# Attention scores on TensorE: three bf16 parts against two float32r parts, and the constant fills moved

## The chip, the cores and the metric

The kernel runs on one core of a Trainium2 chip. The metric is the device time of one execution in microseconds (us). TensorE (PE) does matrix products, VectorE (DVE) and ScalarE (ACT) do elementwise work and reductions and read TensorE's results from PSUM, GpSimd (POOL) does elementwise work and issues the indirect transfers, and SyncE (SP) issues nearly all other DMAs, one after the other in the order of its program.

## The reference

One layer on x of 4 x 1024 x 128 (float32): half a mixture of experts, attention, and half the same mixture again.

```python
x = x + 0.5 * ffn(layernorm(x), W1, b1, W2, b2, Wr, br)      # top-1 of 8 experts
x = x + attn(layernorm(x), Wq, bq, Wk, bk, Wv, bv, Wo, bo)   # 16 heads of 8
x = x + 0.5 * ffn(layernorm(x), W1, b1, W2, b2, Wr, br)

def attn(x, ...):
    q = (x @ Wq + bq).reshape(B, S, 16, 8).transpose(0, 2, 1, 3)   # k and v alike
    scores = einsum('bhsd,bhtd->bhst', q, k) / sqrt(8)
    ctx = einsum('bhst,bhtd->bhsd', softmax(scores), v)
    return ctx.transpose(0, 2, 1, 3).reshape(B, S, 128) @ Wo + bo
```

The softmax needs each row's maximum before its exponentials; the kernel computes all scores twice, once for the maxima and once for the exponentials.

## The kernel before

Five stages follow each other: the front (norm, routing of the 4096 tokens to experts, `Front`), the first expert stage (`Tiles`: 32 tiles of 128 sorted tokens, gathered and scattered by GpSimd's indirect DMAs), attention (`attention`), and routing and experts again.

**Precision.** A matmul of bf16 keeps 8 bits of a number, so query and key are each cut into three bf16 parts (`PARTS = 3`). All nine products of parts are summed in one matmul by putting them side by side on the contracted rows: 9 x 8 = 72 rows (`ROWS`) for one head. The maxima use 64 of them (`MAX_ROWS`); the exponentials' scores use 72, and two more rows, the guards, that hold minus the maximum of the query's row in two parts, against ones in the key's tile. For even heads of a group the rows start at partition 0 and the score matmul contracts 74 rows; for odd heads the maxima's rows start at 64 and the score matmul contracts all 128 rows, where the spare rows are constants: zeros in the query's tile `q2`, ones in the key's `k2`. Those constants, and ones in the value tile `vs`, are written by 12 memsets on GpSimd (`gpsimd_fill`, 4 for each of 3 buffers), one behind each of the first 12 scatters of the first expert stage.

**Making the parts.** Tokens come in 8 quads of 512. For each quad and for query and key ACT writes the first part (`high_part`), DVE or POOL the remainder (`remainder`, `remainders`), ACT the second part (`second_part`), DVE or POOL the third (`third_part`). SP stores them in HBM (`store_query`, `store_key`), the key's three times over, and loads them again per group of 4 heads (`load_queries`, `load_keys`, 10 DMAs a group). The parts of a quad live in one of `SPLITS = 3` buffers; ACT's `high_both(q)` waits until the stores of quad q - 3 have landed.

**The softmax.** There are 16 groups of 4 heads (`GROUPS`), each with 16 steps, 256 steps in all. In a step PE does two maxima units (each two matmuls of 512 columns into one `ps_m` bank pair, on rows 0-63 and 64-127), scores 0, 1 and 2 of the step (into the three banks `ps_s`), the values of the step before (four f32 matmuls of 32 output partitions each, into `ps_o`), and score 3. DVE reduces each maxima unit (`maxima_unit`), ACT does four exponentials. The maxima run 22 units ahead (`AHEAD`), so units for a later half stand in each of the first 245 steps, and the first 22 units are done in the prologue, among the projections of the quads (`prologue`). Score n waits until exponential n - 3 has freed its bank; a maxima unit waits until the unit two before it is reduced; the values of a step wait for all four exponentials of it.

**Guards.** After 16 units (a half of a group, 8 steps) the maxima go round: DVE `combine`, POOL `split_maxima`, DVE `turn_maxima` (behind the second unit of the next half), then SP `place_guard`: a DMA to HBM, a wait for it to land, and two DMAs into `q2`. PE waits for them (`in_m`) at the start of each eighth step, ahead of that step's first unit. Which rows the names mean: `ps_m<-k,q` are maxima units, `ps_s<-q,k` scores, `ps_o<-probs,vs` values.

Of the kernel before, what the change touches and what calls it, by code (L numbers as in the profile page):

```python
# [4 lines left out]
F32 = mybir.dt.float32  # L5
BF16 = mybir.dt.bfloat16
I32 = mybir.dt.int32
# [6 lines left out]
P = 128  # L14
# [21 lines left out]
PARTS = 3  # L36
ROWS = PARTS * PARTS * DK
MAX_ROWS = ROWS - DK
GUARDS = 2
SCORED = ROWS + GUARDS  # L40
# [70 lines left out]
class Setup:  # L111
# [69 lines left out]
    FILLED = 4 * BUFS  # L181
    PAIR = float(0x3f803f80 - 0x3f800000) / 2 ** 23 + 1.0

    def gpsimd_fill(self, pool, n):

        p, piece = n // 4, n % 4
        if n:
            pool.wait_ge(self.filled, n)
        if piece == 0:
            self.nc.gpsimd.memset(self.k2[p][64:96, 0::2, :].bitcast(F32), self.PAIR).then_inc(self.filled, 1)  # L190
        if piece == 1:
            self.nc.gpsimd.memset(self.k2[p][0:64, 1::2, :].bitcast(F32), self.PAIR).then_inc(self.filled, 1)
        if piece == 2:
            self.nc.gpsimd.memset(self.q2[p][0:64, 1::2, :].bitcast(F32), 0.0).then_inc(self.filled, 1)
        if piece == 3:
            self.nc.gpsimd.memset(self.vs[p][:, :, :, :], 1.0).then_inc(self.filled, 1)
# [241 lines left out]
class Front:  # L438
# [121 lines left out]
    def gpsimd(self, pool):  # L560
        self.setup.gpsimd_masks(pool)
        for q in self.BY_POOL:
# [4 lines left out]
            last.then_inc(self.normed_pool, 1)  # L567
        pool.wait_ge(self.route.stored, 2 * 16 * QUADS)
# [3 lines left out]
class Tiles:  # L572
# [68 lines left out]
    def gpsimd(self, pool):  # L641
# [246 lines left out]
SPLITS = 3  # L888
# [59 lines left out]
def attention(nc, w, dram, q2, k2, vs, v_sb, ctx_sb, front, tiles, routes_2):  # L948
# [9 lines left out]
    with ExitStack() as ctx:  # L958
# [10 lines left out]
        exact, rem = probs[:, :, 0:2, :], probs[:, :, 2:4, :]  # L969
# [3 lines left out]
        parts = sb("parts", [P, SPLITS, 2, PARTS, HALF], BF16)  # L973
        parts_flat = parts[:, :, :, :, :].rearrange("p a j m c -> p (a j m c)")
# [8 lines left out]
        split = sb("split", [P, 2, GUARDS, GH // 2 * QUAD], BF16)  # L983
        blocks = [sb(f"blocks{p}", [P, 4 * KT], BF16) for p in range(2)]
# [17 lines left out]
        x_loaded, middle, query_stored, normed_act = tiles.setup.x_load, sem("middle"), sem("query_stored"), front.normed_act  # L1002
        left, low = sems("left", FIRST + 1), sems("low", FIRST + 1)
        LAST = QUADS - 1

        LOADS, STORES = 2 * PARTS + 1 + 3, 1 + PARTS

# [6 lines left out]
        def product(j, n, m=0):  # L1014

            row = (n * PARTS + m) * DK
            return row if j == 0 else MAX_ROWS + row if row < MAX_ROWS else row - MAX_ROWS

        def guard(j):
# [804 lines left out]
```

## Time and profile before

| what | value |
|---|---|
| device time, median of 3 runs | 999.62 us (999.19 to 999.98) |
| span of the profiled execution | 996.9 us (the profile gives this execution's span; its own time is not listed apart from the three above, whose median is 2.7 us above the span) |
| PE, DVE, ACT, POOL busy | 91%, 83%, 75%, 22% of the span |
| largest groups | DVE reductions of maxima 602.8 us, ACT exponentials 555.9 us, PE scores 294.5 us, PE values 272.7 us, PE maxima 159.9 us |

A busy share says only how full an engine is; which one sets the pace has to be read from what each engine waits for in the stretch in question.

### The profile page before, as it was taken

What the parts mean: (1) busy time and instruction counts of PE and PEld (TensorE: products, weight loads), DVE (VectorE), ACT (ScalarE), POOL (GpSimd) and SP (SyncE); (2) the same over time, 40 slices, a digit from 0 to 9 for tenths busy, and PEclk for the clock granted to TensorE, in tenths of its full rate; (3) what the DMA queues carried; (4) which work ended last, traced back from release to release, by engine and by line L of the source; (5) the groups of instructions that cost most, each with busy time, mean ns of one, the idle gap of its engine ahead of it and who ended that gap; (6) DMA issues with size and microseconds to landing.
All of it is one profiled execution on the core that took longest, in us unless ns stands there. A gap on an engine that the chain in (4) does not pass through costs nothing. (4 is left out here: it accounts for less than half of the span.)

```text
span 996.9 us, 18005 instructions
## 1 busy us (share of the span) xinstructions
PE 907.5 (91%) x5949; PEld 385.6 (39%) x6023; DVE 832.2 (83%) x1404; ACT 750.2 (75%) x1507; POOL 219.1 (22%) x317
## 2 busy tenths in 40 slices
PE   5799927899999999999999999999999999965996
PEld 4699923322222222222222222222222222434996
DVE  6776628989999999999999999999999998768664
ACT  4367706978888888888888888888888888754774
POOL 3168841831000000000000100000100000024775
PEclk9989957999999999999999999999999999996998
DMA  7632135752220213202022120220202000051311
GB/s 262 194 96 73 41 116 190 238 192 63 58 61 16 62 34 81 62 17 62 15 73 74 31 62 15 73 54 28 75 30 64 29 23 17 2 169 48 105 63 44
DMA packets 65443, 75.14 MB, mean 75 GB/s; under 512 B 12896, under 2 KB 43784, under 8 KB 65352
## 3 DMA queue, kind: packets, MB, share of 16 engines
q1 hardware_dynamic: 58776, 60.98, 20.6%
q0 software_dynamic: 5120, 12.59, 4.1%
q8 instruction: 51, 0.84, 0.3%
q10 hardware_dynamic: 1456, 0.41, 0.2%
q14 instruction: 40, 0.33, 0.1%
HBM read 40.47 MB, written 33.49 MB: 74 GB/s over the span
## 5 line engine op out<-in xcount | busy, mean ns | idle before, releaser
L1574 DVE TENSOR_REDUCE maxima<-ps_m 128x2 f32<-128x1024 f32 x512 | 602.8, 1221 | 53.8 <-PE ps_m L1335 52.8
L1544 ACT ACTIVATE probs<-ps_s 128x512 f32<-128x512 f32 x1024 | 555.9, 600 | 109.5 <-PE ps_s L1381 77.7
L1381 PE MATMUL ps_s<-q,k 74*128 74x512 bf16 (+1 forms) x950 | 294.5, 385 | 3.0 <-ACT probs L1544 0.9
L1392 PE MATMUL ps_o<-probs,vs 128*32 128x512 f32 x2048 | 272.7, 605 | 0.7 <-ACT probs L1544 0.7
L1381 PEld LDWEIGHTS ps_s<-q,k 74*128 74x128 bf16 (+1 forms) x1024 | 79.5, 97 | 303.4 <-ACT probs L1544 217.1
L1335 PE MATMUL ps_m<-k,q 64*128 64x512 bf16 x1024 | 159.9, 385 | 13.8 <-ACT probs L1544 7.9
L1265 POOL TENSOR_SCALAR split<-top 128x16 bf16<-128x16 f32 x32 | 8.1, 253 | 445.8 <-DVE top L1590 428.7
L1335 PEld LDWEIGHTS ps_m<-k,q 64*128 64x128 bf16 x1024 | 49.1, 93 | 102.7 <-issue 58.1
L693 PE MATMUL ps_y<-W,hT 128*128 x624 | 83.8, 278 | 0.0
L1392 PEld LDWEIGHTS ps_o<-probs,vs 128*32 128x32 f32 x2048 | 40.3, 108 | 109.3 <-issue 95.1
L693 PEld LDWEIGHTS ps_y<-W,hT 128*128 128x128 f32 x624 | 77.0, 194 | 0.6 <-issue 0.4
L647 POOL DMA_INDIRECT v_and_ctx<-token_rows,source_i x64 | 61.7, 964 | 68.0 <-POOLq L1132 22.4
L732 ACT ACTIVATE w1s<-W 128x644 f32 (+1 forms) x78 | 57.5, 739 | 6.7 <-DVE begun L804 6.0
L746 ACT ACTIVATE hT<-ps_ha,w1s 128x128 f32<-128x128 f32 x156 | 48.3, 365 | 8.6 <-PE ps_hb L681 8.6
L849 DVE TENSOR_SCALAR hT<-ps_hb,w1s 128x128 f32<-128x128 f32 x156 | 47.5, 346 | 5.8 <-PE ps_hb L681 2.3
L681 PE MATMUL ps_ha<-xsT,w1s 128*128 (+1 forms) x312 | 49.8, 284 | 1.4 <-ACT w1s L732 1.4
L681 PE MATMUL ps_hb<-xsT,w1s 128*128 (+1 forms) x312 | 49.3, 282 | 0.0
L863 DVE SCALAR_TENSOR_TENSOR v_and_ctx<-y_sum,half_mask,v_and_ctx 128x128 f32 x78 | 27.5, 353 | 21.2 <-DVE y_sum L858 21.2
L681 PEld LDWEIGHTS ps_ha<-xsT,w1s 128*128 128x128 f32 x312 | 42.8, 199 | 2.0 <-issue 1.9
L681 PEld LDWEIGHTS ps_hb<-xsT,w1s 128*128 128x128 f32 x312 | 42.9, 199 | 0.0
L722 ACT ACTIVATE xsT<-ps_x 128x128 f32<-128x128 f32 x64 | 17.7, 277 | 32.6 <-PE ps_x L672 32.1
L858 DVE TENSOR_TENSOR y_sum<-ps_y,w1s 128x128 f32<-128x128 f32 x78 | 22.8, 292 | 22.3 <-PE ps_y L693 21.7
(215 smaller groups left out, 586.3 us busy)
## 6 DMA issues: line engine op xcount, KB each, us to landing
k_rows<-parts SPq DMA_DIRECT2D x24, 384.0 KB, 4.5
sums<-oT SPq DMA_DIRECT2D x30, 256.0 KB, 3.6
q<-q_parts SPq DMA_DIRECT2D x75, 96.0 KB
k<-k_rows SPq DMA_DIRECT2D x15, 288.0 KB
token_rows<-x SPq DMA_DIRECT2D x16, 256.0 KB, 4.1
token_rows<-v_and_ctx SPq DMA_DIRECT2D x16, 256.0 KB, 3.6
k<-k_rows SPq DMA_DIRECT2D x15, 256.0 KB
q_parts<-parts SPq DMA_DIRECT2D x8, 384.0 KB, 3.4
```

Of the source, the lines that this page charges most:

```text
L647: nc.gpsimd.indirect_dma_start(self.xs[:, t, :], None, self.dram["token_rows"], bass.IndirectOffsetOnAxis(ap=self.routes.source_i[:, t:t + ...
L681: last = nc.tensor.matmul(self.ps_h[c // 2][i % 2][:, (c % 2) * P:(c % 2 + 1) * P], self.w1s[:, i % W_ROTATION, c * P:(c + 1) * P], self.x ...
L693: last = nc.tensor.matmul(self.ps_y[i % 2][:, 0:D], self.hT[:, i % 2, c * P:(c + 1) * P], w["W2"][:, bass.ds(e, 1), c, :].rearrange("p a d ...
L732: nc.scalar.activation(self.w1s[:, i % W_ROTATION, 0:width], w["W1"][:, bass.ds(e, 1), 0:width].rearrange("p a h -> p (a h)"), ACT.Copy).t ...
L746: last = nc.scalar.activation(self.hT[:, i % 2, c * P:(c + 1) * P], self.ps_h[0][i % 2][:, c * P:(c + 1) * P], ACT.Relu, bias=self.w1s[:, ...
L849: last = nc.vector.tensor_scalar(self.hT[:, i % 2, c * P:(c + 1) * P], self.ps_h[1][i % 2][:, (c - 2) * P:(c - 1) * P], self.w1s[:, i % W_ ...
L863: nc.vector.scalar_tensor_tensor(out=row, in0=self.y_sum[:, i % 2, :], scalar=self.half_mask[:, i:i + 1], in1=row, op0=ALU.mult, op1=ALU.a ...
L1335: last = nc.tensor.matmul(ps_m[slot][:, j % 2, :], q2[buffer(g)][rows, j, qt * P:(qt + 1) * P], k2[buffer(g)][rows, j, kh * HALF:(kh + 1) ...
L1381: nc.tensor.matmul(ps_s[n % 3][:, :], k2[buffer(g)][0:contracted, j, kt * P:(kt + 1) * P], q2[buffer(g)][0:contracted, j, u * HALF:(u + 1) ...
L1392: last = nc.tensor.matmul(ps_o[32 * j:32 * (j + 1), :], vs[buffer(g)][:, kt, j, :], probs[:, s % 2, j, :], start=(kt == 0), stop=(kt == KT ...
L1544: nc.scalar.activation(probs[:, s % 2, j, :], ps_s[n % 3][:, :], ACT.Exp, scale=SCALE).then_inc(exped, 1)
L1574: nc.vector.tensor_reduce(maxima[:, :, pr, qt, kh], ps_m[slot][:, :, :], AX.X, ALU.max).then_inc(unit_free[slot], 1)
```

## The change

Queries and keys are cut into two parts of type float32r (a four-byte type that TensorE multiplies at less than full f32 precision) in place of three of bf16 (`PARTS = 2`). Four products of 8 rows make 32 rows. Each head now owns one half of PE's rows: 32 product rows, 30 spare rows of constants, and the two guards in the half's last two rows. The maxima contract 62 rows, the scores 64, both in halves 0 and 64. With all heads in halves, the tiles `q2` and `k2` hold pairs of heads ([128, 2, 1024] of four bytes in place of [128, 4, 1024] of two).

The second part is the remainder itself, so `second_part` and `third_part` are gone. The key's parts are stored once, and repeated by the loads (12 DMAs a group). There are `SPLITS = 2` part buffers, so `high_both(q)` waits for the stores of quad q - 2. The fills are 9 memsets over whole tiles, and stand in the front, ahead of the gathers. In a step PE does one unit, scores 0 and 1, the other unit, score 2, values, score 3. SP places the first guard ahead of all stores of quad 5, where before the first of that quad's four stores came ahead of it.

```diff
-PARTS = 3
+PARTS = 2
 ROWS = PARTS * PARTS * DK
-MAX_ROWS = ROWS - DK
+ODD = P // 2
 GUARDS = 2
-SCORED = ROWS + GUARDS
+GUARD = ODD - GUARDS
+SCORED = GUARD + GUARDS
...
-SPLITS = 3
+SPLITS = 2
...
+            self.nc.gpsimd.memset(self.k2[p][:, :, :].bitcast(F32), 1.0).then_inc(self.filled, 1)
...
+            self.nc.gpsimd.memset(self.q2[p][:, :, :].bitcast(F32), 0.0).then_inc(self.filled, 1)
...
+        pool.wait_ge(self.normed_pool, len(self.BY_POOL))
+        for n in range(self.setup.FILLED):
+            self.setup.gpsimd_fill(pool, n)
         pool.wait_ge(self.route.stored, 2 * 16 * QUADS)
         pool.wait_ge(self.route.routed, Route.FOUND)
...
         for t in range(TILES):
             scatter(t)
-            if self.setup and t < self.setup.FILLED:
-                self.setup.gpsimd_fill(pool, t)
...
+                for n in range(PARTS):
+                    for m in range(PARTS):
+                        row = product(j, n) + m * DK
+                        engine.dma_start(k[row:row + DK, :, tokens].bitcast(F32), k_rows[n, :, :, :]).then_inc(landed, 16)
...
                 load(1)
                 store(QUADS - 4)
-                store_key(sp, QUADS - 3, 0)
                 place_guard(0)
-                store_rest(QUADS - 3)
-                for q in range(QUADS - 2, QUADS):
+                for q in range(QUADS - 3, QUADS):
                     store(q)
...
-                    for j in (2 * pr, 2 * pr + 1):
-                        rows = slice(j % 2 * MAX_ROWS, (j % 2 + 1) * MAX_ROWS)
+                    for j in range(2):
+                        rows = slice(j * ODD, j * ODD + GUARD)
...
-                    u, kt, n, contracted = k // KT, k % KT, GH * (STEPS * g + k) + j, (P if j % 2 else SCORED)
+                    u, kt, n, rows = k // KT, k % KT, GH * (STEPS * g + k) + j, slice(j % 2 * ODD, j % 2 * ODD + SCORED)
...
-                    for unit in units:
+                    for unit in units[:1]:
                         do_unit(*unit)
-                    for j in range(GH - 1):
+                    for j in range(2):
                         score(g, k, j)
+                    for unit in units[1:]:
+                        do_unit(*unit)
+                    score(g, k, 2)
                     if s:
                         values(s - 1)
                     score(g, k, GH - 1)
```

The steady softmax on PE, before (`ps_m` maxima, `ps_s` scores, `ps_o` values; one step runs from a `ps_m` row to the next pair of them):

```order
L1335 MATMUL ps_m0<-k2_0,q2_0 128x512 x2
L1335 MATMUL ps_m1<-k2_0,q2_0 128x512 x2
L1381 MATMUL ps_s0<-q2_2,k2_2 128x512
L1381 MATMUL ps_s1<-q2_2,k2_2 128x512
L1381 MATMUL ps_s2<-q2_2,k2_2 128x512
L1392 MATMUL ps_o<-probs,vs2 32x512 x4
L1381 MATMUL ps_s0<-q2_2,k2_2 128x512
```

And of the change:

```order
L1307 MATMUL ps_m0<-k2_0,q2_0 128x512 x2
L1353 MATMUL ps_s2<-q2_0,k2_0 128x512
L1353 MATMUL ps_s0<-q2_0,k2_0 128x512
L1307 MATMUL ps_m1<-k2_0,q2_0 128x512 x2
L1353 MATMUL ps_s1<-q2_0,k2_0 128x512
L1364 MATMUL ps_o<-probs,vs0 32x512 x4
L1353 MATMUL ps_s2<-q2_0,k2_0 128x512
```

The second unit moved behind scores 0 and 1.

SP's queue around the first guard, before (quads 4 and 5 of the prologue; `k_rows` and `q_parts` are the stores of the parts):

```order
L1067 DMA k_rows<-parts 128x3x512 [waits high]
L1143 DMA guards<-blocks 4x32x32 [waits turned_maxima]
L1147 DMA q_0<-guards 2x2x512 [waits guards_out]
L1147 DMA q_0<-guards 2x2x512
L1055 DMA q_parts<-parts 128x3x512 [waits low2]
L1067 DMA k_rows<-parts 128x3x512 [waits middle]
```

And of the change, where the first two rows are quad 4's stores:

```order
L1050 DMA q_parts<-parts 128x2x512 [waits left2]
L1057 DMA k_parts<-parts 128x2x512 [waits left2]
L1124 DMA guards<-blocks 4x32x32 [waits turned_maxima]
L1128 DMA q_0<-guards 2x2x512 [waits guards_out]
L1128 DMA q_0<-guards 2x2x512
L1050 DMA q_parts<-parts 128x2x512 [waits left2]
```

Every store of quad 5 now stands behind the guard's round trip, as two of its three parts did before.

POOL from the front to the scatters, before (`v_and_ctx<-token_rows` are gathers, `x_rows<-v_and_ctx` scatters):

```order
L565 TENSOR_SCALAR v_and_ctx<-x,mv,rt 128x128 x8
L647 DMA v_and_ctx<-token_rows,source_i 128x256 x32
L654 DMA x_rows<-v_and_ctx,source_i 4096x128
L190 MEMSET k_0 32x2x512
L654 DMA x_rows<-v_and_ctx,source_i 4096x128
L192 MEMSET k_0 64x2x512
```

And of the change (three of the nine memsets):

```order
L565 TENSOR_SCALAR v_and_ctx<-x,mv,rt 128x128 x8
L192 MEMSET k_0 128x2048
L194 MEMSET q_0 128x2048
L196 MEMSET vs 128x1024
```

The memsets moved from between the scatters to ahead of the first gather.

## Rows read from the trace of the kernel before

**Rows 1.** Stretch, its us, busy us of PE, PEld, DVE, ACT, POOL, clock, DMA.

```profile
400.00:500.00 100.00, 98.39 (x604) 25.01 (x612) 91.36 (x88) 84.64 (x159) 4.59 (x18) 1.00 0.16 41
```

**Rows 2.** Group of reductions, 300 to 700 us: busy us, mean ns, idle before.

```profile
L1574 DVE TENSOR_REDUCE maxima<-ps_m 128x2 f32<-128x1024 f32 x306 | 360.5, 1220 | 32.3 <-PE ps_m L1335 31.7
```

**Rows 3.** Timeline of one softmax step (start us, length us).

```profile
503.15 0.39 PE L1381 MATMUL ps_s<-q,k 128*128 128x512 bf16 x1
503.47 0.62 PE L1335 MATMUL ps_m<-k,q 64*128 64x512 bf16 x4
503.90 2.36 DVE L1574 TENSOR_REDUCE maxima<-ps_m 128x2 f32<-128x1024 f32 x2 [0.26 <-PE ps_m L1335]
504.02 0.83 PE L1381 MATMUL ps_s<-q,k 74*128 74x512 bf16 x3
504.51 1.57 ACT L1544 ACTIVATE probs<-ps_s 128x512 f32<-128x512 f32 x3 [0.34 <-PE ps_s L1381]
504.77 1.07 PE L1392 MATMUL ps_o<-probs,vs 128*32 128x512 f32 x8
505.77 0.10 PEld L1381 LDWEIGHTS ps_s<-q,k 128*128 128x128 bf16 x1 [0.84 <-ACT probs L1544]
```

**Rows 4.** Timeline, the first step: a score that waited for an exponential.

```profile
202.33 2.06 ACT L1544 ACTIVATE probs<-ps_s 128x512 f32<-128x512 f32 x4 [3.16 <-DVE parts L1103]
202.98 0.39 PE L1381 MATMUL ps_s<-q,k 128*128 128x512 bf16 x1 [0.36 <-ACT probs L1544]
```

**Rows 5.** Timeline, one half's guards: the turn, SP's DMAs, PE's steps.

```profile
406.51 0.20 DVE L1598 STREAM_TRANSPOSE blocks<-split 128x32 bf16<-128x32 bf16 x1
...
424.79 0.62 PE L1335 MATMUL ps_m<-k,q 64*128 64x512 bf16 x4
427.50 0.20 DVE L1598 STREAM_TRANSPOSE blocks<-split 128x32 bf16<-128x32 bf16 x1
432.67 0.61 PE L1335 MATMUL ps_m<-k,q 64*128 64x512 bf16 x4 [0.26 <-ACT probs L1544]
```

**Rows 6.** Timeline: a step start released by the guards' landing.

```profile
222.70 0.31 PEld L1335 LDWEIGHTS ps_m<-k,q 64*128 64x128 bf16 x4 [0.23 <-DMA q<-guards]
```

**Rows 7.** Timeline: an f32 matmul of 512 columns; 48 f32 weight loads.

```profile
190.08 1.12 PE L1419 MATMUL ps_s<-den,Wq 128*128 128x512 f32 x2
32.77 5.43 PEld L222 LDWEIGHTS ps_l<-W,relu_b 128*128 128x128 f32 x48
```

**Rows 8.** Timeline of POOL: front, fills among scatters, last scatters.

```profile
18.66 3.42 POOL L565 TENSOR_SCALAR v_and_ctx<-x,mv,rt 128x128 f32<-128x128 f32 x4 [1.71 <-DVE shift L490]
44.00 1.20 POOL L647 DMA_INDIRECT v_and_ctx<-token_rows,source_i  x1 [21.92 <-DVE source_i L435]
87.61 1.02 POOL L654 DMA_INDIRECT x_rows<-v_and_ctx,source_i  x1 [0.30 <-issue]
113.14 0.98 POOL L654 DMA_INDIRECT x_rows<-v_and_ctx,source_i  x1 [0.17 <-issue]
137.71 0.98 POOL L654 DMA_INDIRECT x_rows<-v_and_ctx,source_i  x1 [0.30 <-issue]
```

**Rows 9.** Timeline at the end of the expert stage and the start of attention; a memset's length.

```profile
126.49 0.35 DVE L863 SCALAR_TENSOR_TENSOR v_and_ctx<-y_sum,half_mask,v_and_ctx 128x128 f32 x1 [0.26 <-DVE y_sum L858]
140.27 3.67 SPq L1199 DMA_DIRECT2D x<-x_rows  x8
95.02 0.98 POOL L196 MEMSET vs<- 128x1024 f32 x1
```

**Rows 10.** Timeline of the prologue: first reduction, first guard, last quad.

```profile
167.99 2.59 DVE L1574 TENSOR_REDUCE maxima<-ps_m 128x2 f32<-128x1024 f32 x2 [1.41 <-PE ps_m L1335]
191.89 0.20 DVE L1598 STREAM_TRANSPOSE blocks<-split 128x32 bf16<-128x32 bf16 x1
196.14 0.69 ACT L1492 ACTIVATE parts<-ps_s,bq 128x512 bf16<-128x512 f32 x1
201.25 0.61 PE L1335 MATMUL ps_m<-k,q 64*128 64x512 bf16 x4 [0.94 <-DVE v_and_ctx L1652]
```

More of the change, by code:

```diff
@@ L6 @@
 BF16 = mybir.dt.bfloat16
+F32R = mybir.dt.float32r
 I32 = mybir.dt.int32
@@ L1012, in use, with product @@
             return g // BUFS
[L1014 to L1019, printed above, removed]
-            return ROWS if j == 0 else DK
+        def product(j, n):
+            return j % 2 * ODD + n * PARTS * DK
         def load_queries(engine, g, landed, tokens=slice(0, SEQ)):
@@ L1289, in _ @@
                         split_maxima(0)
-                    for j in range(2):
-                        third_part(pool, nc.gpsimd, q, j)
                     if q == FIRST:
@@ L1500, in high_both @@
                         high_part(q, j)
-                def second_part(q, j):
-                    parts_done(act, left, q, j + 1)
-                    nc.scalar.activation(parts[:, q % SPLITS, j, 1, :], rem[:, q % 2, j, :], ACT.Copy).then_inc(middle, 1)
                 front.scalar(act)
@@ L1532, in _ @@
                         normalise(q + 2)
-                    for j in range(2):
-                        second_part(q, j)
-                parts_done(act, low, LAST - 1, 2)
-                parts_done(act, low, LAST, 2)
+                parts_done(act, LAST - 1, 2)
                 for s in range(SOFT):
@@ L1684, in remainder @@
                     dve.wait_ge(high, high_parts(q) + j + 1)
-                    nc.vector.scalar_tensor_tensor(out=rem[:, q % 2, j, :], in0=bank[:, :], scalar=bias[:, 0:1], in1=parts[:, q % SPLITS, j, 0, :],
-                                                   op0=ALU.add, op1=ALU.subtract).then_inc(left[q % LAST], 1)
+                    nc.vector.scalar_tensor_tensor(out=parts[:, q % SPLITS, j, 1, :].bitcast(F32R), in0=bank[:, :], scalar=bias[:, 0:1],
+                                                   in1=parts[:, q % SPLITS, j, 0, :], op0=ALU.add, op1=ALU.subtract).then_inc(left[q % LAST], 1)
                 front.vector(dve)
@@ L1723, in _ @@
                     values(late.pop(0))
-                for j in range(2):
-                    third_part(dve, nc.vector, LAST, j)
                 for s, units in enumerate(SCHEDULE):
@@ L1769, in layer @@
         }
-        q2, k2 = ([sb(f"{n}{p}", [P, GH, SEQ], BF16) for p in range(BUFS)] for n in ("q2_", "k2_"))
+        q2, k2 = ([sb(f"{n}{p}", [P, GH // 2, SEQ], F32R) for p in range(BUFS)] for n in ("q2_", "k2_"))
         vs = [sb(f"vs{p}", [P, KT, GH, 32], F32) for p in range(BUFS)]
```

110 lines of the change are left out of this document (38 added, 72 removed).

## The prediction

> **What bounds the kernel now.** I read the windows first. In the steady softmax PE is busy 98.4 of 100 us, DVE 91.4, ACT 84.6, all at the full clock of 2.4 GHz [rows 1]. Then the groups: DVE idles between its reductions, and what ends the idle is PE [rows 2]. So PE sets the pace of a step, and DVE is close behind. The timeline of one step says how PE spends it [rows 3]. From score 3 at 503.15 to the next at 505.77 are 2.62 us: 0.32 from score 3 to the first unit, 0.55 for two units (503.47 to 504.02), 0.75 for three scores (to 504.77), 1.00 for the values. Three scores end 0.83 after the first starts and one takes 0.39, so the pitch of a 512-column bf16 matmul is 0.22. Six pitches (score 3, two units whose two matmuls run side by side in the row halves, three scores) make 1.32 of the 1.62 outside the values; the remaining 0.30 are three seams, where the shape of PE's tiles changes between 64 rows, 128 rows and 128 x 32. A fourth seam lies inside the 1.00.
>
> Behind PE stand two more limits. DVE needs 2.36 for two reductions [rows 3]; 306 of them took 360.5 us, 1.18 each [rows 2]. And the guards: turns lie 20.99 apart (406.51, 427.50), eight steps; from the turn at 427.50 to the eighth step's first unit at 432.67 are 5.17 [rows 5]. That step did not visibly wait for the guards, but another did: its weight load was released by the guards' DMA [rows 6]. The round trip is thus as long as PE happens to take, and has no slack for a faster PE.
>
> The first expert stage ends with POOL: the last DVE result is at 126.49, the x loads of attention start only at 140.27 [rows 9], because the last scatter is issued at 137.71 [rows 8].
>
> **Fills: removed from the scatters, added in the front.** Scatters 13 to 32 take (137.71 - 113.14)/19 = 1.29 each; the first twelve, with fills between them, (113.14 - 87.61)/12 = 2.13 [rows 8]. Without fills the last scatter would be issued at 87.61 + 31 x 1.29 = 127.6, and its data is complete from 126.84 (126.49 + 0.35) [rows 9], just in time. I take **-10.1 us**. The bounds are 0 and -10.9 (it cannot start before its data). In the front, a memset of 1024 columns took 0.98 [rows 9]; nine memsets hold 15 x 1024 columns, 14.7 us, plus nine gaps of at most 0.2, 16.5 in all. POOL is idle from 22.08 to 44.00, when the routing releases the gathers [rows 8]. They end by 38.6 and cost nothing; were that cover gone, they would cost up to 16.5.
>
> **Part-making in the prologue.** Second and third parts vanish from ACT, DVE and POOL, and quads 0 and 1 reach SP earlier by about one ACT and one DVE pass each. That brings the first maxima unit nearer by up to 3 us; DVE then needs the same 22 reductions. Against it stands a wait that the change adds. Turn 0 comes 23.9 after the first reduction (167.99 to 191.89), quad 7's first part 28.2 after it (196.14), step 0 33.3 after it (201.25) [rows 10]. Now ACT's first part of quad 7 must wait for both stores of quad 5, which stand in SP's queue behind turn 0, its DMA out, the landing and the DMAs in. In the steady guards the whole trip is 5.17 [rows 5]; of this I take a third, 1.7, for the last landing, so the queue is free some 3.5 after the turn, and two stores of 512 KB issue and land in about 5 (an estimate, from the 5.17 that a DMA out, its landing and two DMAs in take). That is 23.9 + 3.5 + 5 = 32.4 after the first reduction, 4.2 later than today. Behind it wait quad 7's remainders on DVE, the values of quads 6 and 7 queued behind those, and step 0. With 3 gained and 4.2 lost I take **+1.3**, with bounds of -3 (the stores are in time) and +6.
>
> **The step.** The unknown is a float32r matmul of 512 columns; no row shows one. The bounds are the bf16 pitch, 0.22 [rows 3], and full f32: 1.12 for a pair of records that ends in the same latency of 0.39 - 0.22 = 0.17, so 0.95 at most [rows 7], with 0.88 as four bf16 pitches. I choose 0.22: the change rounds both operands to fewer bits, so that one piece of each is left to multiply, as with bf16, and it is the bf16 row that multiplies one piece by one. The Trainium skill ("FP8 and Floating Point Precision", TensorE Precision Notes) says that reduced-precision FP32 is read as four bytes and cut to 22 bits, while true FP32 takes four passes; by the first the pitch would be 0.22, by the second four times that.
>
> With that pitch, three sums for a step:
> - PE's work. Score 3 (half 64), unit (0, 64), score 0 (0), score 1 (64), unit (0, 64), score 2 (0): eight half-array matmuls, four pitches, 0.88; values to the next score 3 1.00; one seam into the values 0.08 (0.30 from score 2 to the values less 0.22). 1.96.
> - DVE: two reductions, 2.36, and 0.4 a half for combining and turning: 2.41.
> - The loop through ACT, as score 2 waits for exponential 3 of the step before, and the values stand behind score 2. Values to score 3 1.00, score 3 to its exponential 0.49 (504.02 to 504.51), that exponential and its release 0.65 (202.33 to 202.98 [rows 4]), score 2 to the values 0.30: **2.44** [rows 3].
>
> So the loop is now the longest: 2.62 to 2.44. But the guards take part back. Of eight steps, three (turn's half) are not paid by PE's pace: step 5's first unit to the turn is 2.71 (424.79 to 427.50), turn to guards 5.17 [rows 5]; together 7.88, three of today's steps. Check for today: 5 x 2.62 + 7.88 = 20.98. With the change, the step behind the wait is short (1.96, its exponentials are done), four follow at 2.44, then 7.88: 19.6. DVE's count for the same stretch: 0.43 to the first reduction, 12 x 1.18, 0.2 and 5.17 give 19.96, which is longer. I take 20.0, **-0.98 a half**. Turns 0 to 31 are 31 halves apart, and the last has few units; 30 x 0.98 = **-29.4 us**. At an infinitely fast PE nothing more would come, since DVE and the guards' trip are left; at 2.44 in all steps with no guard wait it would be 19.5 a half, -44.
>
> Weight loads: a bf16 load is recorded at 0.10 [rows 3], and 48 f32 loads of 128 columns took 5.43, 0.113 each [rows 7]. Eight a step are 0.90 at 0.113, hidden behind 0.88 of streaming or 0.02 over; the seam ahead of score 3 may grow by 0.05. Even 0.1 more in the loop leaves 2.54 and a half at 20.1. The Trainium skill ("TensorE: Matmul & The Clock Gate", Fast Weight Load) says that the fast load is off for FP32 weights; then eight loads at its columns/1.2 GHz would be 0.85 by its figure, hidden too.
>
> The last 11 steps and everything behind are the same work: 0.
>
> **Sum.** 996.9 - 10.1 + 1.3 - 29.4 = 958.7 of span, and the median lies 2.7 above the span: **961 us**.
>
> **Rivals.**
> - *Somewhat dearer float32r* (a pitch of 0.27, or exposed loads): PE 2.16, loop 2.54, a half 2.16 + 4 x 2.54 + 7.9 = 20.2, to 20.7 if DVE's waits add up: -8 to -23 there, 967 to 982. Chance 0.10. For it: no row shows the type.
> - *The guards' trip grows* with four-byte rows or with 12 loads in SP's queue (10 today) by 0.5 to 1: 15 to 30 back, 976 to 991. Against it: latency, not bytes, makes most of the 5.17. Chance 0.05.
> - *Weight loads bound PE, slower.* If the loads of the two halves exclude each other and each takes twice the 0.113, eight make 1.81 in place of 0.88 and a step 1.81 + 1.08 = 2.89, a half 5 x 2.89 + 7.9 = 22.3 to 8 x 2.89 = 23.1: +40 to +64, less the 8.8 gained before: 1031 to 1055. It decides from 0.20 a load, where a half is 21.3. Against it: the 0.113 itself [rows 7]. Chance 0.05.
> - *Float32r costs two or four pitches, slower.* Two: 8 x 0.22 + 1.08 = 2.84 a step, 22.1 to 23.1 a half, +34 to +64: 1025 to 1055. Four: 4 x 0.88 + 1.08 = 4.60, 36.8 a half, +474: about 1465. Chance 0.09 together. From a pitch of 0.35 (step 2.48, loop 2.70, a half 21.3) the change loses.
> - *Nothing gained in the softmax*, the guards holding all of it, leaves 991. Chance 0.02.
> - Forecast: 0.69, own range 950 to 972.
>
> No change would be within 0.2% (2 us) of 999.6, about what the runs can tell. Faster: 0.69 + 0.10 + 0.05 + 0.02 = 0.86, of which I leave 0.02 for errors on the fills' cover; same 0.02; slower 0.14. The range takes the forecast's, the dearer pitch and the longer trip: 948 to 990; below it stands 955 if the guards' wait is hidden in part and the prologue gains its 3, above it only the slower cases.
>
> **What the profile after would show.** Nine memsets between 22 and 38 us and scatters 1.29 apart from the first; x loads at about 130. Step 0 near 192, with ACT's first part of quad 7 idle ahead of it on a DMA. Score records of 64 rows at 0.39, two starting together; steps of 2.44, PE below 90% busy; every eighth step a wait of PE for the guards' DMA of about 0.8; turns 20.0 apart. The prediction is wrong if the float32r records are longer than 0.39 plus 0.1, if PE's weight loads stand end to end, if turns lie more than 20.7 apart, or if the memsets push the first gather past 44.

## The result, and the profile after

The changed kernel took 993.1 us (median of 4 runs, 990.9 to 994.9), the kernel before, timed beside it, 999.8 (4 runs): a ratio of 0.9932, 95% interval 0.9910 to 0.9954. It is faster by 0.7%, where 961 us had been forecast (3.9% faster). The profiled execution has a span of 992.4 us against 996.9.

Three marks cut both spans into stretches: the first reduction of maxima, the first exponential of the softmax, and the end of its last exponential.

| stretch, us | before | after | difference |
|---|---|---|---|
| start to first reduction | 167.99 | 155.24 | -12.75 |
| first reduction to first exponential | 34.34 | 39.01 | +4.67 |
| first to end of last exponential | 673.86 | 674.39 | +0.53 |
| behind it | 120.7 | 123.8 | +3.1 |

All that was gained was gained ahead of the softmax. The last line has little to do with the change: the same stretch took 120.7, 123.9 in two profiles of the kernel before, and 120.5, 123.0 in two of it with only the fills moved; where it is long, the clock falls as attention ends. Two windows behind the softmax show it (stretch, its us, busy us of PE, PEld, DVE, ACT, POOL, granted clock, DMA), of after and of the kernel before in its second profile (e15):

```profile
875.00:880.00 5.00, 4.93 (x24) 4.25 (x24) 3.42 (x16) 1.69 (x3) 2.96 (x4) 0.57 0.79 233
```

```profile
880.00:885.00 5.00, 4.23 (x20) 3.69 (x19) 3.42 (x12) 0.69 (x3) 4.68 (x6) 0.50 0.67 195
```

The kernel before does it too, now and then: 0.50 of full speed is the level of 1.2 GHz. In its first profile no window from 865 to 890 was below 1.00.

The timeline of the front and of the scatters, after (start us, length us):

```profile
22.03 1.81 POOL L192 MEMSET k<- 128x2048 f32 x1
...
35.23 0.95 POOL L196 MEMSET vs<- 128x1024 f32 x1
44.42 1.20 POOL L650 DMA_INDIRECT v_and_ctx<-token_rows,source_i  x1 [8.24 <-DVE source_i L435]
...
88.00 1.02 POOL L657 DMA_INDIRECT x_rows<-v_and_ctx,source_i  x1 [0.30 <-issue]
...
128.19 0.98 POOL L657 DMA_INDIRECT x_rows<-v_and_ctx,source_i  x1 [0.30 <-issue]
130.77 1.29 SPq L1175 DMA_DIRECT2D x<-x_rows  x3
```

The nine memsets end at 36.2, and the first gather still waits for the routing (44.42, against 44.00 in [rows 8]). The 31 gaps between the scatters are 1.30 each. The last scatter is issued at 128.19 (137.71 in [rows 8]), the x loads start at 130.77 (140.27 in [rows 9]): 9.5 us gained.

The prologue, from the first reduction to the first exponential, after:

```profile
155.24 2.48 DVE L1538 TENSOR_REDUCE maxima<-ps_m 128x2 f32<-128x1024 f32 x2 [1.66 <-PE ps_m L1307]
...
179.16 0.20 DVE L1562 STREAM_TRANSPOSE blocks<-split 128x32 f32<-128x32 f32 x1
179.40 0.63 SPq L1124 DMA_DIRECT2D guards<-blocks  x1
181.44 1.32 SPq L1128 DMA_DIRECT2D q<-guards  x2
182.81 0.40 SPq L1050 DMA_DIRECT2D q_parts<-parts  x1
183.25 0.47 SPq L1057 DMA_DIRECT2D k_parts<-parts  x1
187.17 0.69 ACT L1467 ACTIVATE parts<-ps_s,bq 128x512 fp32r<-128x512 f32 x1 [5.20 <-DMA k_parts<-parts]
189.96 2.07 PE L1387 MATMUL ps_o<-Wv,den 128*128 128x128 f32 x8 [4.43 <-DVE v_and_ctx L1616]
192.97 0.79 PE L1307 MATMUL ps_m<-k,q 62*128 62x512 f32 x2 [0.94 <-issue]
194.25 2.08 ACT L1508 ACTIVATE probs<-ps_s 128x512 f32<-128x512 f32 x4 [5.81 <-PE ps_s L1353]
```

Quad 5's stores go out at 182.81 and 183.25, behind the guard's round trip. ACT waits 5.20 us for their landing before quad 7, and everything behind it follows late. After the 4.43 us in which PE idled, its eight matmuls take 2.07 us where eight took 1.16 at 176.06: they run at the lower clock (a granted clock of 0.50 from 190 to 196 us, the level of 1.2 GHz, and 1.00 again from 200 us).

A step of the steady softmax, after (PE, its weight loads and ACT; [rows 3] has the same of before):

```profile
501.64 0.50 PE L1353 MATMUL ps_s<-q,k 64*128 64x512 f32 x1
...
502.18 2.07 ACT L1508 ACTIVATE probs<-ps_s 128x512 f32<-128x512 f32 x4 [0.55 <-PE ps_s L1353]
...
502.83 0.18 PEld L1353 LDWEIGHTS ps_s<-q,k 64*128 64x128 f32 x1 [0.42 <-ACT probs L1508]
502.83 0.49 PE L1353 MATMUL ps_s<-q,k 64*128 64x512 f32 x1
503.25 1.06 PE L1364 MATMUL ps_o<-probs,vs 128*32 128x512 f32 x8
504.24 0.18 PEld L1353 LDWEIGHTS ps_s<-q,k 64*128 64x128 f32 x1 [0.84 <-ACT probs L1508]
...
504.78 2.06 ACT L1508 ACTIVATE probs<-ps_s 128x512 f32<-128x512 f32 x4 [0.54 <-PE ps_s L1353]
```

A step is 2.60 (502.18 to 504.78, in other steps 2.61). It is one closed chain, counting a step's scores and exponentials from 0 to 3: exponential 3 of the step before starts at 502.18, its bank is free and score 2 starts at 502.83 (0.65), the values at 503.25 (0.42), score 3 at 504.24 (0.99), its exponential at 504.78 (0.54). The window of the steady softmax and the waits of 300 to 700 us show two things that mislead or rule out:

```profile
400.00:500.00 100.00, 99.75 (x613) 38.43 (x610) 91.07 (x86) 81.49 (x158) 4.00 (x16) 1.00 0.25 50
```

```profile
PEld ps_s L1353 <- ACT probs L1508: 191.0, 320, 0.8
...
PEld ps_m L1307 <- DMA q<-guards: 2.3, 7, 0.6
```

PE is busy 99.75 of 100 us (98.39 in [rows 1]), which looks like an engine at its limit; whether it is, e2 and e13 below decide. And the guards hold PE for only 2.3 us in 400, so the trip of [rows 5] is not what is left.

The page's groups of after, busy us and mean ns of one:

```profile
L1353 PE MATMUL ps_s<-q,k 64*128 64x512 f32 x1024 | 372.7, 448 | 0.2
L1353 PEld LDWEIGHTS ps_s<-q,k 64*128 64x128 f32 x1024 | 167.5, 185 | 326.8 <-ACT probs L1508 317.1
```

### The profile page after: what moved, and what is told of

Its sections match the earlier page's. It is cut to its first block and busy times, and to the rows that moved or that the text cites. A ratio compares the mean times of both kernels' runs of the same rounds, so it can differ in the third digit from the quotient of the medians.

```text
span 992.4 us, 18055 instructions
## 1 busy us (share of the span) xinstructions
PE 925.7 (93%) x6023; PEld 480.5 (48%) x6023; DVE 828.8 (84%) x1398; ACT 721.8 (73%) x1491; POOL 211.6 (21%) x304
## 5 line engine op out<-in xcount | busy, mean ns | idle before, releaser
L1508 ACT ACTIVATE probs<-ps_s 128x512 f32<-128x512 f32 x1024 | 535.0, 603 | 133.6 <-PE ps_s L1353 129.4
L1353 PE MATMUL ps_s<-q,k 64*128 64x512 f32 x1024 | 372.7, 448 | 0.2
L1353 PEld LDWEIGHTS ps_s<-q,k 64*128 64x128 f32 x1024 | 167.5, 185 | 326.8 <-ACT probs L1508 317.1
L1307 PE MATMUL ps_m<-k,q 62*128 62x512 f32 x1024 | 300.1, 447 | 3.1 <-issue 0.9
L1307 PEld LDWEIGHTS ps_m<-k,q 62*128 62x128 f32 x1024 | 121.5, 185 | 29.9 <-DVE maxima L1538 9.7
L1239 POOL TENSOR_SCALAR split<-top 128x16 fp32r<-128x16 f32 x32 | 8.1, 253 | 451.3 <-DVE top L1554 428.0
```

The costliest lines, as they stand in the source:

```text
L1307: last = nc.tensor.matmul(ps_m[slot][:, j, :], q2[buffer(g)][rows, pr, qt * P:(qt + 1) * P], k2[buffer(g)][rows, pr, kh * HALF:(kh + 1) * ...
L1353: nc.tensor.matmul(ps_s[n % 3][:, :], k2[buffer(g)][rows, j // 2, kt * P:(kt + 1) * P], q2[buffer(g)][rows, j // 2, u * HALF:(u + 1) * HAL ...
L1508: nc.scalar.activation(probs[:, s % 2, j, :], ps_s[n % 3][:, :], ACT.Exp, scale=SCALE).then_inc(exped, 1)
```

## The experiments

Two theories of the step of after stand against each other. The first (L): the step is held by the loop exponential 3, score 2, values, score 3, and in it two float32r weight loads lie bare. The rival (P): PE has more work in all, because float32r is dearer everywhere. The sixteen experiments came on four chips, four on each (e1 to e4 on the 1st; which chip the first two rows of the table came from is not recorded); each ratio is to the kernel before on the same chip. "Half" is the mean distance of turns 1 to 31 (eight steps), the other columns are stretches of the profiled execution. In the expectations of the last eight runs the stretch "from the first to the last exponential" reaches to the last of the routing that follows attention, 14 to 18 us later and not the same in each run; by that mark before has 688.4 us, after 691.3, e1 669.0, e3 663.3. Where the two marks differ in what they say, the table's is the one of the softmax.

| kernel | us (runs) | ratio, 95% interval | reduction to exponential | first to last exponential | half |
|---|---|---|---|---|---|
| before | 999.8 | 1 | 34.3 | 673.9 | 20.95 |
| after | 993.1 | 0.993 (0.991 to 0.995) | 39.0 | 674.4 | 20.90 |
| e1_scores_b16 | 974.6 (4) | 0.974 (0.971 to 0.977) | 38.9 | 654.5 | 20.29 |
| e2_maxima_b16 | 993.5 (4) | 0.993 (0.990 to 0.996) | 38.6 | 675.5 | 20.90 |
| e3_both_b16 | 966.8 (4) | 0.968 (0.964 to 0.971) | 38.6 | 646.4 | 20.03 |
| e4_fills | 990.0 (4) | 0.990 (0.987 to 0.992) | 35.1 | 673.5 | 20.96 |
| e5_guard_later (2nd chip) | 1044.8 (10) | 0.996 (0.993 to 0.999) | 35.1 | 676.2 | 20.92 |
| e6_six (2nd) | 1005.3 (4) | 0.959 (0.956 to 0.963) | 34.3 | 631.5 | 19.58 |
| e7_six_order (2nd) | 1007.5 (4) | 0.959 (0.956 to 0.962) | 34.1 | 636.1 | 19.69 |
| e8_six_loads (2nd) | 1006.7 (4) | 0.960 (0.957 to 0.964) | 34.2 | 631.3 | 19.57 |
| e9_both_b16_loads (3rd) | 1024.0 (4) | 0.972 (0.967 to 0.977) | 39.6 | 644.8 | 19.99 |
| e10_f32_order (3rd) | 1058.6 (10) | 1.004 (1.002 to 1.006) | 39.3 | 676.5 | 20.94 |
| e11_guard_loads (3rd) | 1050.5 (10) | 1.000 (0.997 to 1.003) | 35.4 | 675.1 | 20.92 |
| e12_after_again (3rd) | 1056.4 (10) | 1.004 (1.001 to 1.007) | 39.1 | 676.0 | 20.95 |
| e13_first_two_b16 (4th) | 992.9 (4) | 0.992 (0.990 to 0.994) | 39.0 | 674.2 | 20.93 |
| e14_last_two_b16 (4th) | 976.7 (4) | 0.977 (0.974 to 0.980) | 38.9 | 657.5 | 20.36 |
| e15_before_again (4th) | 1000.0 (10) | 0.999 (0.997 to 1.001) | 34.6 | 673.8 | 20.95 |
| e16_fills_again (4th) | 989.3 (4) | 0.989 (0.987 to 0.992) | 34.2 | 674.3 | 20.97 |

### The type alone: e1, e2, e3

```diff
+        def upper(tile, rows, pair, first, count):
+            return tile[rows, pair, first:first + count].bitcast(BF16)[:, 1::2]
...
-                    nc.tensor.matmul(ps_s[n % 3][:, :], k2[buffer(g)][rows, j // 2, kt * P:(kt + 1) * P],
-                                     q2[buffer(g)][rows, j // 2, u * HALF:(u + 1) * HALF], start=True, stop=True).then_inc(scored, 1)
+                    nc.tensor.matmul(ps_s[n % 3][:, :], upper(k2[buffer(g)], rows, j // 2, kt * P, P),
+                                     upper(q2[buffer(g)], rows, j // 2, u * HALF, HALF), start=True, stop=True).then_inc(scored, 1)
```

This is e1; e2 does it to the maxima, e3 to both. `upper` reads the upper two bytes of each number, so the smaller part of queries and keys is left out.

> Only the scores (not the maxima) read the upper two bytes of each four-byte number, as bf16, from the same tiles, in the same order; so the scores lose precision, and nothing else changes. Theory L (the loop through ACT holds the step, and the change lengthened it by the four-byte weight loads that stand exposed ahead of scores 2 and 3): a score after a wait is 0.39 long and not 0.50, score 3 to its exponential falls from 0.54 to 0.49, score 2 to the values from 0.42 to 0.30, the step from 2.61 to 2.44, turns from 20.92 to about 20.0, time about 993 - 28 = 965. Rival P (PE's whole work, all loads and streams, holds the step): half of the float32r work is gone, step about 2.53, time about 980. Rival G (the guards' round trip holds each half): turns stay at 20.9 and the time at 993.

> Only the maxima read the upper two bytes as bf16; the scores stay float32r. The maxima become approximate, which the softmax allows. Theory L: nothing of the loop changes, the step stays at 2.61, turns at 20.9, time 991 to 994. Rival P: step about 2.53, time about 980. Rival G: 993.

> Scores and maxima both read the upper two bytes as bf16. Theory L: as with the scores alone, 2.44 a step, turns about 20.0, about 965, and here PE's own work is 1.96, so that PE waits for ACT ahead of score 2. Rival P: step 2.45, about 968, clearly below the kernel with the scores alone. Rival G: 993.

With bf16 scores the half falls to 20.29; with bf16 maxima, the same number of matmuls made cheaper, nothing moves. e1 took 974.6 us, between L's 965 and P's 980, so its time alone decides nothing. Its step is L's, 2.41 in the median. What is missing is in the guards: from 230 to 850 us PE's weight loads wait 25.7 us for them (3.0 in after), in nearly every half, and two halves take 22.5 and 22.6.

That the maxima's type is worth nothing holds for a step of 2.61. With the scores in bf16 already, it brings another 7.8 us (e3 against e1), which L did not expect: most of e3's halves are 19.8 against 19.9 at best in e1, and none is over 21.1. No run separates why. In e3 too the halves above 19.8, up to 21.05, hold a guard that is late. SP's queue in one of these:

```profile
435.61 1.73 SPq L1028 DMA_DIRECT2D q<-q_parts  x4
437.38 2.71 SPq L1038 DMA_DIRECT2D k<-k_parts  x8
440.13 0.35 SPq L1138 DMA_DIRECT2D sums<-oT  x1
448.25 0.65 SPq L1140 DMA_DIRECT2D v_and_ctx<-sums  x1
448.94 0.55 SPq L1127 DMA_DIRECT2D guards<-blocks  x1
```

SP waits 7.8 us for the sums to land behind the twelve loads, and the guard stands behind that.

### The two halves of the scores: e13, e14

```diff
+                    if j < 2:
+                        keys = upper(k2[buffer(g)], rows, j // 2, kt * P, P)
+                        queries = upper(q2[buffer(g)], rows, j // 2, u * HALF, HALF)
+                    else:
+                        keys = k2[buffer(g)][rows, j // 2, kt * P:(kt + 1) * P]
+                        queries = q2[buffer(g)][rows, j // 2, u * HALF:(u + 1) * HALF]
...
```

This is e13; e14 has `j >= 2`.

> After, with scores 0 and 1 of each step read as bf16 (the upper two bytes of each number, so their smaller part is left out) and scores 2 and 3 in float32r. The loop runs from the exponential of score 3 to score 2 (its buffer comes free), the values, score 3 and its exponential again: scores 0 and 1 are not in it. Loop theory: nothing moves, step 2.60 to 2.62 us, turns 20.9 apart, first to last exponential 690 to 694 us. Rival, TensorE's total work: half of what e1 gained, step 2.51 to 2.52, turns 20.1 to 20.4, stretch 678 to 683.

> The other half: scores 2 and 3 read as bf16 (their smaller part left out), 0 and 1 in float32r. Loop theory: all of e1's gain, step 2.41 to 2.44 us (0.65 + 0.33 + 1.00 + 0.43), turns 19.9 to 20.5 apart, first to last exponential 667 to 672 us. Rival, TensorE's total work: half of it, step 2.51 to 2.52, stretch 678 to 683.

Scores 0 and 1 bring nothing (half 20.93, stretch by the expectations' mark 691.2), scores 2 and 3 most of what e1 brought (20.36 where e1 has 20.29, stretch 672.0; by the table's mark 16.9 of e1's 19.9 us). TensorE's work in all is cut alike in both, so P is out and L stands for the steady steps. The loop's rows in e14:

```profile
501.44 2.07 ACT L1516 ACTIVATE probs<-ps_s 128x512 f32<-128x512 f32 x4 [0.40 <-PE ps_s L1362]
...
502.09 0.09 PEld L1362 LDWEIGHTS ps_s<-q,k 64*128 64x128 bf16 x1 [0.22 <-ACT probs L1516]
502.09 0.40 PE L1362 MATMUL ps_s<-q,k 64*128 64x512 bf16 x1
502.42 0.16 PEld L1372 LDWEIGHTS ps_o<-probs,vs 128*32 128x32 f32 x8 [0.24 <-issue]
502.42 1.06 PE L1372 MATMUL ps_o<-probs,vs 128*32 128x512 f32 x8
503.41 0.09 PEld L1362 LDWEIGHTS ps_s<-q,k 64*128 64x128 bf16 x1 [0.84 <-ACT probs L1516]
503.42 0.40 PE L1362 MATMUL ps_s<-q,k 64*128 64x512 bf16 x1
503.85 0.60 ACT L1516 ACTIVATE probs<-ps_s 128x512 f32<-128x512 f32 x1 [0.35 <-PE ps_s L1362]
```

0.65 + 0.33 + 0.99 + 0.44 = 2.41. Against after, each of the two scores is 0.10 shorter (0.40 for 0.50), and its weight load 0.09 (0.09 for 0.18). The record of a just released score starts together with its load, so 0.09 of the 0.10 is the load. This is read from the records: no run changed the type of the load alone. In e13 the two scores of the loop, still float32r, keep 0.18 and 0.50:

```profile
503.59 0.18 PEld L1362 LDWEIGHTS ps_s<-q,k 64*128 64x128 f32 x1 [0.40 <-ACT probs L1516]
503.60 0.50 PE L1362 MATMUL ps_s<-q,k 64*128 64x512 f32 x1
504.02 0.16 PEld L1372 LDWEIGHTS ps_o<-probs,vs 128*32 128x32 f32 x8 [0.25 <-ACT probs L1516]
```

### The order of PE's work: e10

```diff
-                    for unit in units[:1]:
+                    for unit in units:
                         do_unit(*unit)
-                    for j in range(2):
+                    for j in range(GH - 1):
                         score(g, k, j)
-                    for unit in units[1:]:
-                        do_unit(*unit)
-                    score(g, k, 2)
```

> After with TensorE's work of a step in the order of the kernel before: both units, three scores, the values of the step before, the last score. Score 3 still follows the values and the values still follow score 2, both with a float32r weight load at the seam, so the loop theory expects the same step, 2.60 to 2.64 us, turns 20.8 to 21.1 apart, and a whole within 4 us of after. If the new order had won something (or lost something) of its own under float32r, turns change by 0.3 us or more and the whole by 10 us or more.

The half is 20.94 against 20.95 in e12 beside it, and the time 1.002 of it: under float32r the order of the units is worth nothing, as L expected of work that isn't in the loop.

### The rows without float32r: e6, e7, e8

```diff
-MAX_ROWS = ROWS - DK
+ODD = P // 2
 GUARDS = 2
-SCORED = ROWS + GUARDS
+GUARD = ODD - GUARDS
+SCORED = GUARD + GUARDS
...
-            row = (n * PARTS + m) * DK
-            return row if j == 0 else MAX_ROWS + row if row < MAX_ROWS else row - MAX_ROWS
+            return j % 2 * ODD + sum(PARTS - i for i in range(n)) * DK
```

The bf16 kernel with the rest of the change: three parts, six products in 48 rows of a half, guards in its last two rows. e7 is e6 in before's order; e8 moves the loads.

> The kernel before, with the twelve fills in the front, and in place of nine products of bf16 parts the six largest (48 rows, so that a head fits in one half of TensorE's rows with its two guard rows); TensorE's work in a step is in the order of after. Left out are the three smallest products (middle by least, least by middle, least by least). Theory L, the loop exponential - score 3 - exponential is the bound and float32r's weight loads and pitch lengthened it: step 2.41 to 2.44 us, turns 19.8 to 20.0 apart where no guard is late, scores' record 0.40, whole 958 to 966 us. Rival, that full halves or spare rows cost something of their own (mode switches between 64 and 128 rows): step 2.55 to 2.62, whole 980 to 992 us.

> The same as e6_six, with TensorE's work of a step in the order of the kernel before (both units' maxima and scores first, values behind). If the loop through score 3 is the bound whatever the order, the step is again 2.41 to 2.46 us and the whole within 3 us of e6_six. If the order of after brought part of the shorter step, the step is 2.50 to 2.62 and the whole 12 to 30 us over e6_six.

> e6_six with each group's loads of queries and keys moved behind the guard of the half that they were ahead of, so that the sums' transfer and the guard are not queued behind the loads. If guards that come late behind the loads are what makes some turns 20.6 to 21 apart instead of 19.8, the long turns go and the whole falls 4 to 8 us below e6_six. If the loads then come late for the next group, turns of the next group grow and it is as slow or slower; if the long turns come from elsewhere, within 2 us of e6_six.

e6 is the fastest version, 4.1% under before: halves of 19.58, the softmax 42 us shorter. Its own step, on ACT:

```profile
502.11 2.07 ACT L1539 ACTIVATE probs<-ps_s 128x512 f32<-128x512 f32 x4 [0.33 <-PE ps_s L1373]
...
504.50 2.06 ACT L1539 ACTIVATE probs<-ps_s 128x512 f32<-128x512 f32 x4 [0.32 <-PE ps_s L1373]
```

2.39 a step. e7's time is within the runs' spread of e6, but its softmax is 4.6 us longer and its half 19.69, so with bf16 the order of after seems worth a little (one profile of each). The times themselves (1005) missed the expected 958 to 966, because this chip took more in every kernel (below); the steps and halves are as expected, and 0.959 of 999.8 would be 959. e8 gains nothing: from 230 to 850 us PE's weight loads wait 18.4 us for guards in it and 18.8 in e6.

### The fills, the first guard, the loads: e4, e5, e9, e11, e12

e4 is the kernel before with this part of the change alone:

```diff
+        for n in range(self.setup.FILLED):
+            self.setup.gpsimd_fill(pool, n)
...
-            if self.setup and t < self.setup.FILLED:
-                self.setup.gpsimd_fill(pool, t)
```

e5 is after with quad 5's stores ahead of the first guard, e9 is e3 with the second edit, and e11 is after with both:

```diff
                 store(QUADS - 4)
+                store(QUADS - 3)
                 place_guard(0)
-                for q in range(QUADS - 3, QUADS):
+                for q in range(QUADS - 2, QUADS):
                     store(q)
```

```diff
-                    if 1 <= g < GROUPS - 2:
-                        sp.wait_ge(step_done, STEPS * g)
-                        load(g + 2)
...
                     place_guard(2 * g + 1)
...
-                    if g == 0:
-                        load(2)
+                    if g < GROUPS - 2:
+                        wait_unless_zero(sp, step_done, STEPS * g)
+                        load(g + 2)
```

> The kernel before with one part of the change alone: its 12 fills in the front, ahead of the gathers. All theories: they fit into GpSimd's idle time (12 x 1.0 + gaps, from 22 to about 36 us), the scatters run 1.29 apart, attention starts 9.5 to 10 us earlier: time 990. If the front's fills delay the first gather or the end of the expert stage, less.

> After with one move: the stores of quad 5 are issued ahead of the first guard on GpSimd's queue, not behind it; nothing is left out. If the prologue loses time because ScalarE's quad 7 waits for quad 5's buffer (5.20 us in the profile of after) and TensorE then idles and comes back at 1.2 GHz, this wait goes, scores of step 0 start 3 to 5 us earlier against the first reduction, and the whole takes 988 to 990 us. If the guards' own trip is what step 0 waits for in any case, it stays within 1 us of after (992 to 994). Under both the steps stay at 2.61 us and turns 20.9 apart.

> e3_both_b16 with each group's twelve loads moved behind the guard of the half that they were ahead of. As in e3 only the upper two bytes of each number are read, so the scores' smaller parts are left out. In e3 the turns were 19.8 us apart except for some twelve of 20.4 to 21.1, some 8 us in all, where the guard and the sums' transfer stood behind the loads on the queue. If the queue is the cause, nearly all turns come to 19.8 and the stretch from the first to the last exponential falls from 663 to 655 us or less. If it is not, the long turns stay and the stretch is 661 us or more.

> After with two moves on the queues, nothing left out: quad 5's stores ahead of the first guard, and each group's twelve loads behind the guard of the half that they were ahead of. First reduction to first exponential 35 us as in e5 against 39 in after; the loads' move should bring at most 2 us, since only some four turns of after are longer than 20.93. Whole 3 to 6 us below after on the same chip.

> The changed kernel as it is, so that the other three have it beside them on the same chip. 0.991 to 0.996 of the kernel before, first reduction to first exponential 39 us, turns 20.9 us apart.

e4 takes 990.0, less than the whole change. e5's whole took 1044.8 and not the expected 988 to 990, on a chip where after was not timed, so what the move brings to the whole isn't shown by it; its prologue can be compared. (Its expectation speaks of GpSimd's queue; stores and guard are on SP's.) e5's prologue, where quad 5's stores no longer stand behind the guard:

```profile
184.72 2.36 DVE L1539 TENSOR_REDUCE maxima<-ps_m 128x2 f32<-128x1024 f32 x2 [0.75 <-PE ps_m L1308]
...
208.67 0.69 ACT L1467 ACTIVATE probs<-ps_s,bq 128x512 f32<-128x512 f32 x1 [1.65 <-DMA k_parts<-parts]
...
219.78 2.69 ACT L1509 ACTIVATE probs<-ps_s 128x512 f32<-128x512 f32 x5 [4.82 <-PE ps_s L1354]
```

35.1 from the first reduction to the first exponential: 3.9 of the 4.7 us are that one queue position. Timed beside after on one chip, both moves together (e11) bring 1050.5 against 1056.4, 5.9 us; the stretch to the first exponential accounts for 3.8 of it. e12 itself took 1.004 of the kernel before and missed its 0.991 to 0.996. e9 came out between its two cases: the long halves shrink from eight over 20.3 us in e3 to two, but one of those took 23.2 and the stretch, 659.3 by the expectations' mark, fell by 4.0 from e3, not by 8; by the table's mark it fell by only 1.6 (644.8 against 646.4). PE's weight loads still wait 22.4 us for guards from 230 to 850 us, against 26.2 in e3. The queue makes the guards late, and that is not all that does.

### The kernel before on another chip: e15, e16

> The kernel before as it is, profiled beside the others. On a chip like the first: first reduction at 168, first exponential 34.3 us later, stretch to the last exponential 688.4, tail 106. On a chip like the second and third, where the front and the back took 24 to 30 us more in every kernel: 34.3 and 688.4 again, first reduction at 190 to 197, tail 133 to 137. If the fills cost less there, because GpSimd waits for VectorE between its scatters and fills lie in that wait, first reduction is only 4 to 8 us later than with fills in the front.

> The kernel before with the twelve fills in the front, beside e15 on one chip. On a chip like the first: 10 us less, ratio 0.987 to 0.992. On a chip like the second and third, if the fills lie partly in GpSimd's waits: 4 to 8 us less, ratio 0.992 to 0.996; if they cost the same there as on the first, again 10 us.

Both came on a chip like the first and repeat it: the fills bring 10.7 us of the medians here, as e4 brought 10. So what these two were to settle stays open. On the second and third chip the first reduction came at 182 to 191 us in every kernel profiled, all with the fills in the front, where on the others such kernels have it at 154 to 158, and the stretch behind the last exponential took 149 to 154 us, not 120 to 124. One row of e12's waits, 60 to 190 us, that has no like in the first profile of after:

```profile
ACT xsT L723 <- remote: 24.5, 4, 12.9
```

ACT stands in the expert stage for something that the profile can't name. On the third chip after took 1.004 of before, not 0.993, with the softmax and the prologue as in its first profile. What is missing must then be in the front or at the end. GpSimd waits 42 us for DVE results between 40 and 170 us in e12 and 7 in the first profile of after, and in such waits fills could lie for nothing; that is argued, not shown, since no profile of the kernel before on such a chip is there.

## Why the prediction was wrong

By its own steps, against the profiled execution (span forecast 958.7, measured 992.4, +33.7):

- **Fills, -10.1.** Right: -9.5, in the front at no cost, and alone 10 us in e4 and e16. The sign of error "the memsets push the first gather past 44" came true by the letter (44.42), but the memsets end at 36.18 and the gather waits for the routing. On the third chip the whole change was a loss of 0.4%, cause open.
- **Prologue, +1.3.** Right in size and in mechanism: 3.25 gained up to the first reduction (12.75 less 9.5), 4.67 lost behind it (4.2 forecast), through ACT's wait for quad 5's stores; e5 takes 3.9 of it back. Of the 3.25 some 1 is not the parts' doing: from the x loads to the first reduction before took 27.7, after 24.5, and e4, with the fills alone moved, 26.6.
- **Float32r's pitch, 0.22.** Nearly right: two scores one behind the other start 0.24 apart in after (504.59, 504.83), and it didn't matter for the steady step (e2, e13).
- **Three sums for a step, the loop the longest.** Right: the loop through ACT that the text named is what holds the steady step (e2, e13, e14). That PE would be below 90% busy was wrong, 99.75%, because the record of a just released matmul includes its load.
- **The size of the loop, 2.44: this is the step that failed.** "Score 3 to its exponential 0.49" measured 0.54, and "score 2 to the values 0.30" measured 0.42; the loop is 2.61, as long as the old step of 2.62. Both terms were read in [rows 3] from bf16 matmuls, and both contain the weight load of a matmul that has just been released by another engine. Such a load is hidden behind nothing. The text priced loads in [rows 7], 0.113 each, from 48 that follow each other, and let them vanish behind streaming, "even 0.1 more in the loop leaves 2.54"; bare, one takes 0.18 (bf16 0.09), twice in each loop. The true price was in the trace of before: those same 48 loads overlap each other, and one of them takes 190 ns, as their group says (busy us, mean ns of one, idle):

```profile
L222 PEld LDWEIGHTS ps_l<-W,relu_b 128*128 128x128 f32 x48 | 5.4, 190 | 0.1
```

With bf16 in those two places alone the step is 2.41 (e14), against 2.44 forecast. The Trainium skill ("TensorE: Matmul & The Clock Gate", the section on Fast Weight Load and DoubleRow) says that the fast load is off for FP32 inputs and measures it at about twice the speed; 0.18 against 0.09 agrees. The prediction cited that rule, and set its price by throughput rather than by latency.
- **Guards, half 20.0, -29.4.** With the loop at 2.61 the guards' trip no longer ends the half: PE waits 2.3 us for them in 400. The half is 20.90, and 30 halves bring -1.4. This is 28.0 of the 33.7. The arithmetic itself held where its loop did: 20.03 in e3 (20.0 forecast). There the guards' trip does end the halves, with a wait of 0.9 in each (0.8 forecast). The rows of PE's waits for the guards from 300 to 700 us (us in all, times, longest), of e3 and then of e6:

```profile
PEld ps_m L1310 <- DMA q<-guards: 18.1, 20, 1.9
```

```profile
PEld ps_m L1327 <- DMA q<-guards: 12.5, 20, 1.3
```

- **The last steps, 0.** From the last turn to the last exponential 32.6 us against 30.1: +2.5. These steps have matmuls of the output projection where the others have units, and most take 2.86 before and 3.17 after, from the values of one step to those of the next:

```profile
854.89 1.06 PE L1392 MATMUL ps_o<-probs,vs 128*32 128x512 f32 x8
...
857.75 1.07 PE L1392 MATMUL ps_o<-probs,vs 128*32 128x512 f32 x8
```

```profile
860.74 1.06 PE L1364 MATMUL ps_o<-probs,vs 128*32 128x512 f32 x8
...
863.91 1.06 PE L1364 MATMUL ps_o<-probs,vs 128*32 128x512 f32 x8
```

Here all four scores count, not only the last two: such a step takes 3.06 in e13, 3.08 in e14 and 2.97 in e1, and the two halves of the scores add up. The rest of the 33.7 is the 3.1 behind attention, the first half (-0.6), and 0.7 of the fills and prologue.

Of the rivals, "somewhat dearer float32r (...or exposed loads)" named the mechanism and gave it 0.10 of chance and 967 to 982 us; it stopped at 0.1 in the loop where there were 0.17. That the change is faster at all, as forecast, is owed to the fills alone: e4, which has nothing else of it, took 990.0. The end, 991, is that of "nothing gained in the softmax", but its stated cause, the guards, isn't the one. The text's own sign of error, records "longer than 0.39 plus 0.1", came true (0.50), and so did "turns lie more than 20.7 apart" (20.90).

So the large change moved little because its parts cancel: the full halves of rows, with six products for nine and the new order, bring 42 us of softmax with bf16 (e6 against e4), float32r in all matmuls costs 28 of that (after against e3), and what differs between e3 and e6 the other 15. Of these, 13.5 lie in the 30 halves (20.03 against 19.58). Both kernels have twelve loads a group, but of 1024 KB in e3 and 768 in e6; the longest landing of the sums' transfer is 8.1 us against 4.3, and PE's weight loads wait 26.2 us for guards against 18.8 (230 to 850 us). So about half of the 15 is seen as later guards; the rest is open.

## What to carry to other kernels

Where engines take turns, add up the chain of releases, and price each link by the latency of one instruction that was just released, its weight load included; a mean from a run of back-to-back instructions is a throughput and is too low. Before a change of type, ask which matmuls stand right behind a wait, and keep the cheap load there. A busy share of 99.75% doesn't show that an engine is the bound: make some of its work cheaper outside the loop and see whether anything moves. And when the bound is gone, ask what was free again: the maxima's type, worth nothing at 2.61 a step, was worth 7.8 us at 2.41.

## What the runs showed of the hardware

- In after a float32r matmul of 64 rows by 512 columns is recorded at 0.40 us when its load is hidden (scores 0 and 1) and at 0.50 when it has just been released (scores 2 and 3); bf16 takes 0.40 in the second case too (e14). Its weight load of 128 columns takes 0.18, a bf16 one 0.09. Where float32r and bf16 matmuls alternate, many float32r records are 0.59 (scores 0 and 1 in e2, units in e1); why is open.
- A bare load counts as PE time: the score at 502.83 and its load start together. PE reads as 99.75% busy in after and 97% in e14 in the same window, and in after its total is not the limit (e2, e13).
- The kernel before took 5% more on two of four chips (1048.7 and 1052.5 against 1000.1 and 1001.2). In e12 against after, the same kernel, 32 us of it lie ahead of the first reduction, 28 behind the softmax and 1.6 in it. A gain of 0.7% on one chip was a loss of 0.4% on another.
